# The bias of layer h in the joint part of a graph kernel: from products on TensorE to a column on ScalarE

## What is computed

```python
h = relu(layernorm(x))                       # x: 50000 x 256
S = h[src]                                   # 50000 edges
for r in (0, 1):                             # two relations
    msg_r = relu(relu(S @ W_r.T + b_r) @ W_r.T + b_r)
msgs = where(edge_type == r, msg_r)
agg  = segment_sum(msgs, dst)                # 50000 x 256
i, f, g, o = split(agg @ W_ih.T + b_ih + b_hh)
c  = sigmoid(i) * tanh(g)
hn = sigmoid(o) * tanh(c)
y  = relu(relu(hn @ W1.T + b1) @ W2.T + b2) @ W3.T + b3
out = x + y
```

## Time and profile before

| | |
|---|---|
| median of 3 runs | 2325.51 us (2324.17 to 2326.10) |
| time of the profiled execution | 2326.91 us |
| its span, first to last instruction | 2325.2 us |
| TensorE busy | 2098.4 us, 90% |
| VectorE busy | 1757.9 us, 76% |
| ScalarE busy | 1628.3 us, 70% |
| GpSimd busy | 1150.3 us, 49% |
| mean granted TensorE clock | 0.958 of full speed |

### The profile page before, as it was taken

The page is one execution under the profiler, slowest core; times in us unless marked ns, Lnnn a source line. Parts: engine busy times, 40 slices in busy tenths (PEclk is TensorE's granted clock), DMA queues, the critical chain, the costliest instruction groups (busy, mean ns, idle before and its releaser), DMA issues.

```text
span 2325.2 us, 51837 instructions
## 1 busy us (share of the span) xinstructions
PE 2098.4 (90%) x14224; PEld 1403.6 (60%) x14225; DVE 1757.9 (76%) x4311; ACT 1628.3 (70%) x3364; POOL 1150.3 (49%) x917
## 2 busy tenths in 40 slices
PE   6858777657999999999999999999999999999996
PEld 5747565545666666666666666666666666445553
DVE  7537655555788888888888888888888877788886
ACT  2437655546878787877878787878778786666663
POOL 0037777777555565555655556555555543100000
PEclk7559989999999999999999999999999999999998
DMA  9955555557699989989898989998988987998886
GB/s 387 425 180 100 98 98 96 98 93 143 124 175 171 167 170 170 172 171 172 167 172 172 174 166 169 171 172 172 167 172 169 174 156 151 182 193 188 188 188 154
DMA packets 400606, 396.90 MB, mean 171 GB/s; under 512 B 263738, under 2 KB 343158, under 8 KB 394360
## 3 DMA queue, kind: packets, MB, share of 16 engines
q0 software_dynamic: 91200, 157.34, 42.6%
q1 hardware_dynamic: 306788, 238.12, 40.0%
q10 hardware_dynamic: 2516, 0.14, 0.1%
HBM read 185.88 MB, written 156.97 MB: 147 GB/s over the span
## 4 chain that ended last, share of the span: by engine, by line
PE 43%; ACT 25%; issue 16%; POOL 6%; DVE 5%; DMA 4%; another core or an unknown queue 1%; POOLq 0%; SPq 0%; ACTq 0%; DVEq 0%
PE bank L1469 21%; ACT xn L757 4%; PE bank L1452 4%; PE bank L1483 3%; POOL agg L664 3%; PE bank L1416 3%; POOL xg L648 3%; ACT count_tmp L736 3%; ACT row_hi L790 2%; ACT tcell L783 2%; PE bank L1435 2%; PE bank L1508 2%; ACT g_o L777 2%; PE bank L1398 2%; DMA agg<-summed,scatter_idx 2%
## 5 line engine op out<-in xcount | busy, mean ns | idle before, releaser
L664 POOL DMA_INDIRECT agg<-summed,scatter_idx x400 | 638.2, 1596 | 599.7 <-DVE scatter_idx L1144 454.7
L1469 PE MATMUL bank<-a_hi,ihT 128*128 128x512 f16 x2400 | 715.6, 380 | 4.7 <-DMA a_lo<-row_lo 4.7
L648 POOL DMA_INDIRECT xg<-in_x,src_ring x400 | 416.1, 1040 | 270.2 <-DMA src_ring<-src_slot 137.3
L1469 PE MATMUL bank<-a_lo,ihT 128*128 128x512 f16 x1200 | 455.8, 380 | 0.0
L1469 PEld LDWEIGHTS bank<-a_hi,ihT 128*128 128x128 f16 x2400 | 235.0, 98 | 215.7 <-issue 7.2
L1435 PE MATMUL bank<-relT,h_hi 128*128 x1600 | 322.2, 276 | 0.0
L1416 PE MATMUL bank<-s_hi,relT 128*128 128x256 f16 x1600 | 294.8, 280 | 0.0
L672 POOL DMA_DIRECT2D y<-in_x x100 | 133.2, 1341 | 295.2 <-DVE y L1202 284.3
L777 ACT ACTIVATE g_i<-bank,gate_b 128x512 f32<-128x512 f32 x200 | 137.4, 687 | 138.7 <-PE bank L1469 133.3
L1416 PE MATMUL bank<-s_lo,relT 128*128 128x256 f16 x800 | 223.3, 279 | 0.0
L757 ACT ACTIVATE xn<-xg,shift,rstd 128x256 f32<-128x256 f32 x400 | 216.3, 591 | 9.3 <-DVE shift L1111 9.3
(11 more groups left out here) (197 smaller groups left out, 4647.7 us busy)
## 6 DMA issues: line engine op xcount, KB each, us to landing
agg_in<-agg SPq DMA_DIRECT2D x100, 512.0 KB
y<-in_x POOLq DMA_DIRECT2D x100, 512.0 KB, 6.5
out<-y SPq DMA_DIRECT2D x100, 512.0 KB
agg<-zeros SPq DMA_DIRECT2D x24, 2112.0 KB, 15.9
dst_ring<-dst_rows SPq DMA_DIRECT2D x200, 128.0 KB
xg<-in_x,src_ring POOLq DMA_INDIRECT x400
agg<-summed,scatter_idx POOLq DMA_INDIRECT x400
src_ring<-src_slot SPq DMA_DIRECT2D x200, 1.0 KB
```

Source lines behind the costliest of these rows:

```text
L648: nc.gpsimd.indirect_dma_start(out=xg[:, k.slot(8), t, :], out_offset=None, in_=x[:, :], in_offset=bass.IndirectOffsetOnAxis(ap=src_ring[: ...
L664: nc.gpsimd.indirect_dma_start(out=agg[:, :], out_offset=bass.IndirectOffsetOnAxis(ap=scatter_idx[:, k.slot(8), t:t + 1], axis=0), in_=sum ...
L1469: last = nc.tensor.matmul(N_C[c % 2][:, 0:UNIT], lhs, rhs, start=i == 0, stop=i == len(todo) - 1)
```

## The change

In the joint part `layer_h` no longer opens each half of its bank with a product of `brel_parts` and ones; the first of the six products opens it. ScalarE's `high_h` takes two instructions, one for each half of 256 columns, since the bias differs between them; each adds a bias column and applies the ReLU, and writes f32 to a new tile `h_f`. VectorE makes `h_hi` as a cast of `h_f` (a new `high_h` on VectorE) and `h_lo` as `h_f` less `h_hi`. VectorE's `low_h` moves behind `hidden`, and the new cast stands ahead of `hidden`. The columns are in `pair_bias`, two for each pair, which the set-up makes out of `pair_rel` (now on all 128 partitions) and `brel_col`, loaded by one more DMA on ScalarE's queue. TensorE frees the bank for the next pair on `h_f_ready` instead of `h_ready`. The edge part keeps its bias products. `brel_parts` is still used by layer m.

```diff
-WEIGHT_LOADS = 14
+WEIGHT_LOADS = 15
...
             act.dma_start(brel_row[:, :], b_rel.rearrange("r d -> (r d)").partition_broadcast(2)).then_inc(weights_in, 16)
+            act.dma_start(brel_col[:, :, :], b_rel.rearrange("r (c p) -> p r c", p=P)).then_inc(weights_in, 16)
...
             def high_h(k):
                 if k.within(PAIRS):
                     act.wait_ge(h_done, k.n + 1)
-                    nc.scalar.activation(h_hi[:, k.slot(2), :], B_H[k.bank][:, :], ACT.Relu).then_inc(h_hi_ready, 1)
+                    if k.both:
+                        if k.is_(NB):
+                            act.wait_ge(pair_bias_ready, 1)
+
+                        act.wait_ge(h_ready, k.n)
+                        for m in range(KH):
+                            half = slice(m * PAIR, (m + 1) * PAIR)
+                            last = nc.scalar.activation(h_f[:, half], B_H[k.bank][:, half], ACT.Relu,
+                                                        bias=pair_bias[:, bass.ds(k.n * KH + m, 1)])
+                        last.then_inc(h_f_ready, 1)
+                    else:
+                        nc.scalar.activation(h_hi[:, k.slot(2), :], B_H[k.bank][:, :], ACT.Relu).then_inc(h_hi_ready, 1)
...
-            alternate.then_inc(pair_rel_ready, 1)
+            chained(alternate)
+            nc.vector.tensor_scalar(other_rel[:, :], pair_rel[:, :], 0.0, None, ALU.is_equal).then_inc(pair_rel_ready, 1)
+            dve.wait_ge(pair_rel_ready, 1)
+            dve.wait_ge(weights_in, 16 * WEIGHT_LOADS)
+            for m in range(KH):
+                last = nc.vector.tensor_scalar(other_bias[:, :, m], other_rel[:, :], brel_col[:, 0, m:m + 1], None, ALU.mult)
+            chained(last)
+            bias_of = pair_bias[:, :].rearrange("p (n m) -> p n m", m=KH)
+            for m in range(KH):
+                last = nc.vector.scalar_tensor_tensor(out=bias_of[:, :, m], in0=pair_rel[:, :], scalar=brel_col[:, 1, m:m + 1],
+                                                      in1=other_bias[:, :, m], op0=ALU.mult, op1=ALU.add)
+            last.then_inc(pair_bias_ready, 1)
...
             def low_h(k):
                 if k.within(PAIRS):
-                    dve.wait_ge(h_hi_ready, k.n + 1)
-                    nc.vector.scalar_tensor_tensor(out=h_lo[:, k.slot(2), :], in0=B_H[k.bank][:, :], scalar=0.0,
-                                                   in1=h_hi[:, k.slot(2), :], op0=ALU.max,
-                                                   op1=ALU.subtract).then_inc(h_ready, 1)
+                    if k.both:
+                        dve.wait_ge(h_hi_ready, k.n + 1)
+                        nc.vector.tensor_tensor(h_lo[:, k.slot(2), :], h_f[:, :], h_hi[:, k.slot(2), :],
+                                                ALU.subtract).then_inc(h_ready, 1)
...
+            def high_h(k):
+                if k.within(PAIRS):
+                    dve.wait_ge(h_f_ready, k.n - NB + 1)
+
+                    wait_from(dve, m_done, k.n - 1)
+                    nc.vector.tensor_copy(h_hi[:, k.slot(2), :], h_f[:, :]).then_inc(h_hi_ready, 1)
...
+                if (at - 1).both:
+                    high_h(at - 1)
+                hidden(k, half)
                 low_h(at - 1)
-                hidden(k, half)
...
-                wait_from(pe, h_ready, k.n if k.both else k.n - 1)
+                if k.is_(NB):
+                    pe.wait_ge(h_ready, k.n)
+                elif k.both:
+                    pe.wait_ge(h_f_ready, k.n - NB)
+                else:
+                    wait_from(pe, h_ready, k.n - 1)
                 for m in range(KH):
                     ps = B_H[k.bank][:, m * PAIR:(m + 1) * PAIR]
-                    nc.tensor.matmul(ps, brel_parts[:, bass.ds(r * D + m * P, P)], ones16[:, :], start=True, stop=False)
+                    if not k.both:
+                        nc.tensor.matmul(ps, brel_parts[:, bass.ds(r * D + m * P, P)], ones16[:, :], start=True, stop=False)
...
-                        last = nc.tensor.matmul(ps, lhs, rhs, start=False, stop=i == len(todo) - 1)
+                        last = nc.tensor.matmul(ps, lhs, rhs, start=k.both and i == 0, stop=i == len(todo) - 1)
```

More of the change, by code:

```diff
@@ L218, in build @@
         spare_row = sb("spare_row", [P, 2])
-        pair_start = sb("pair_start", [1, PAIRS])
+        pair_start = sb("pair_start", [P, PAIRS])
         iota_tile = sb("iota_tile", [P, TILES])
@@ L228, in build @@
         dst_slot = sb("dst_slot", [P, TILES])
-        pair_rel = sb("pair_rel", [1, PAIRS], I32)
+        pair_rel = sb("pair_rel", [P, PAIRS], I32)
+        pair_bias = sb("pair_bias", [P, PAIRS * KH])
         unit_row = sb("unit_row", [1, UNITS], I32)
@@ L243, in build @@
         gate_b = sb("gate_b", [P, 8])
+        brel_col = sb("brel_col", [P, NUM_REL, KH])
         b1_col = sb("b1_col", [P, 1])
@@ L295, in build @@
         quarter_row = tmp("quarter_row", [1, QUARTERS])
-        flips = tmp("flips", [1, 2, PAIRS])
+        flips = tmp("flips", [P, 2, PAIRS])
+        other_rel = tmp("other_rel", [P, PAIRS])
+        other_bias = tmp("other_bias", [P, PAIRS, KH])
         slot = tmp("slot", [ROWS, COLS])
@@ L360, in build @@
         s_lo = sb("s_lo", [P, 2, KH * PAIR], F16)
+        h_f = sb("h_f", [P, KH * PAIR])
         h_hi = sb("h_hi", [P, 2, KH * PAIR], F16)
@@ L401, in build @@
         pair_rel_ready = sem("pair_rel_ready")
+        pair_bias_ready = sem("pair_bias_ready")
         unit_row_ready = sem("unit_row_ready")
@@ L430, in build @@
         h_done = sem("h_done")
+        h_f_ready = sem("h_f_ready")
         h_hi_ready = sem("h_hi_ready")
@@ L1010, in _ @@
                         lanes(i * BATCHES + b)
-            alternate = nc.vector.tensor_scalar(flips[:, 0, :], pair_start[:, :], base_s[0:1, QUARTERS - 1, 0:1], None, ALU.is_ge)
+            alternate = nc.vector.tensor_scalar(flips[:, 0, :], pair_start[:, :], base_s[:, QUARTERS - 1, 0:1], None, ALU.is_ge)
             for n, o in enumerate(range(QUARTERS - 2, -1, -1)):
@@ L1017, in _ @@
                 alternate = nc.vector.scalar_tensor_tensor(out=out_t, in0=pair_start[:, :],
-                                                           scalar=base_s[0:1, o, 1 - o % 2:2 - o % 2], in1=flips[:, n % 2, :],
+                                                           scalar=base_s[:, o, 1 - o % 2:2 - o % 2], in1=flips[:, n % 2, :],
                                                            op0=ALU.is_ge, op1=ALU.subtract)
-            alternate.then_inc(pair_rel_ready, 1)
+            chained(alternate)
[10 more added lines that the diff above has]
+            last.then_inc(pair_bias_ready, 1)
             chained(nc.vector.scalar_tensor_tensor(out=rows_of[:, :, :], in0=sel[0:1, :, :], scalar=float(QROWS),
@@ L1075, in low_h @@
                 if k.within(PAIRS):
-                    dve.wait_ge(h_hi_ready, k.n + 1)
-                    nc.vector.scalar_tensor_tensor(out=h_lo[:, k.slot(2), :], in0=B_H[k.bank][:, :], scalar=0.0,
-                                                   in1=h_hi[:, k.slot(2), :], op0=ALU.max,
-                                                   op1=ALU.subtract).then_inc(h_ready, 1)
+                    if k.both:
[3 more added lines that the diff above has]
+                    else:
+                        dve.wait_ge(h_hi_ready, k.n + 1)
+                        nc.vector.scalar_tensor_tensor(out=h_lo[:, k.slot(2), :], in0=B_H[k.bank][:, :], scalar=0.0,
+                                                       in1=h_hi[:, k.slot(2), :], op0=ALU.max,
+                                                       op1=ALU.subtract).then_inc(h_ready, 1)
+            def high_h(k):
[3 more added lines that the diff above has]
+                    nc.vector.tensor_copy(h_hi[:, k.slot(2), :], h_f[:, :]).then_inc(h_hi_ready, 1)
             def spread_of(k):
```

## The result

| | before | after |
|---|---|---|
| median of 4 runs | 2324.84 us (2322.63 to 2326.10) | 2349.99 us (2346.45 to 2353.19) |
| ratio, 95% interval | | 1.0103 (1.0080 to 1.0125) |
| span of the profiled execution | 2325.2 us | 2351.5 us |

The kernel became slower by 25 us. I had forecast 8 us, with 2349 as the upper edge; the median lies 1 us above it.

What follows compares the result with a forecast made beforehand. TensorE was taken to bound even steps, ScalarE odd ones; -15.4 us (TensorE) and +23.1 (ScalarE), the rest nothing, gave +7.7 us, 2333.2 us. The range ran from 2321 to 2349 us, the forecast's own from 2330 to 2338.

Steps and rivals of the forecast that it cites:

- What bounds the kernel: Joint part: even steps (9.99 us) end on TensorE, odd ones on ScalarE, which shows no idle time from `g_g` to `summed`.
- TensorE's term: Layer h, joint part: two matmuls fewer save 0.217 us in each of 71 even steps, -15.4 us; nothing in odd steps.
- ScalarE's term: Layer h's ReLU cut in two with a bias column: 0.33 us added in each of 70 odd steps, +23.1 us.
- the line through `g_i` and the root at 8 columns: Price of ScalarE's half-tile ReLU with bias: 0.59 and 0.21 us give 0.00075 us a column, so 0.40 us each.
- The errata table: ScalarE reading PSUM: 172 cycles plus one per column; second ReLU adds 143 ns, total -5.4 us; weighed, not followed.
- rival D: ScalarE's ReLU pair adds 0.15 to 0.29 us or partly finds cover: no change that can be told, 2321 to 2330 us; chance 0.22.
- The sign that I had set for being wrong: ScalarE's two ReLU halves following each other in under 0.35 us would show the forecast wrong.
- VectorE's step: VectorE: a cast added and `low_h` moved behind `hidden`, making later helpers 0.68 us late; claimed to cost nothing.
- Rival C: Every fourth step's boundary: ScalarE's table load waits for VectorE's `mean_var`, +24 us on top of 7.7, 2357 us; chance 0.09.
- Cost nothing: Verdict on VectorE's cast and moved `low_h`, on the new waits and on the set-up: no time added.
- A: ScalarE's ReLU pair: the bias column is free, 0.09 us added per odd step, -9.1 us, 2316 us; chance 0.11.
- B: ScalarE's ReLU halves cost what the `xn` pair costs, 0.52 us added per odd step, +21 us, 2346.5 us; chance 0.15.

## Why the prediction was right in its direction, and why its size was a third

*What bounds the kernel: right.* Even steps end on TensorE, odd ones on ScalarE; the runs with even steps only and with the products kept show both halves.

*TensorE's term: right.* Forecast 71 x 0.217 = -15.4 us; even steps went from 9.99 to 9.77.

*ScalarE's term: right in kind, over a third too large.* Forecast 0.33 added, measured 0.71 - 0.47 = 0.24; odd steps became 10.10 and 10.44 in place of 10.19 and 10.52, and the sums waited 0.82 us in place of 0.91. The mis-sized part is the line through `g_i` and the root at 8 columns: half a tile takes 0.71 / 2 = 0.355 us, not 0.40. The slope of 0.00075 us a column was too small: from 512 columns with a bias column (0.57) to 256 (0.355) it is 0.00084. The errata table that I had weighed (the Trainium skill, "VectorE: DVE Perf Modes") is right about the cut: 143 ns by its estimate, 0.14 measured. It has no term for the column, which cost 0.10 here; that is what I had held against it. With the measured price the sum is 70 x 0.24 - 15.4 = +1.4 us, which is rival D's case and not the forecast. The sign that I had set for being wrong here, halves that follow each other in under 0.35 us, was missed by less than 0.01.

*VectorE's step: the times right, the step wrong.* The cast, the move and the late helpers cost nothing in the steps that repeat, as said: the kernel with `low_h` ahead has the same ones. Rival C falls too. Timelines after, of ScalarE and of VectorE at a boundary:

```profile
1237.29 0.69 ACT L815 ACTIVATE x<-bank,b_col 128x512 f32<-128x512 f32 x1
1238.00 1.28 ACT L752 ACT_TABLE_LOAD   x1
1239.29 0.30 ACT L752 ACTIVATE std<-mean_var,eps 128x8 f32<-128x8 f32 x1
```

```profile
1238.27 0.24 DVE L1128 BATCH_NORM_AGGREGATE mean_var<-stats 128x2 f32<-128x6 f32 x2
```

The load starts 0.5 us before `mean_var` ends.

But the verdict "Cost nothing" on VectorE's work was reached by adding up durations, and it left out the number and the place of the instructions. 24 more in the loop and 40 more ahead of it moved its end from 0.20 to 0.70 of 128 behind a multiple, and that cost 21.9 us in 13 turns. No rival of mine had that; it was the step that failed. That the kernel got clearly slower, and that the time came near the upper edge, is luck: it is owed to a cause that I hadn't named. What I had named gives +1.4 us by the measured prices and +4.2 (0.7 to 7.7) by the timed runs without the stalls.

*The sum of the parts.* The spans differ by 26.3 us. The 17 groups of eight steps give 17 x 0.11 = 1.9, the fetching 21.9. Another 1.7 lies in the first eight steps of the joint part (81.83 us, with 11.07 in one step); the runs of the changed kernel with 32, 64 (both) and 128 memsets have that as well (81.81 to 81.85), the one with 192 (80.17) and the one with `low_h` ahead (80.15) have not. What makes it stays open. The rest, 0.8, is from before and after the joint part.

*Rivals.* A (the column is free) falls by 0.10 us. B (as dear as `xn`, 0.99) falls by 0.71. D was right for the change itself: it needed an added time of 0.15 to 0.29, and that was 0.24.

## What to carry to other kernels

Ask in which steps a saving and a cost fall before you add them: here the same edit is worth -0.22 us where TensorE ends the step and +0.24 us where ScalarE does, and doing it in every second step only turned a zero into a gain. When an edit changes the number of instructions ahead of or in a loop, look at the first instruction of the loop for idle time with no releaser and at the packets of the instruction queue, before you look for a cause in the edit; dummy instructions ahead of the loop show in a run or two whether it is the place (64 took the stall away here, 32 and 128 didn't). And a kernel can be slower for its layout alone: the unchanged one got 13 stalls, and 12 us in the steps that have them, from 64 memsets in idle time.

## What the runs showed of the hardware

The stall at the jump back of VectorE's loop depends on the place of the loop with a period of 128 instructions: loops that ended at numbers 1562, 1594, 1690 and 1818 of the program (0.20, 0.45, 0.20 and 0.20 of 128 behind a multiple) had none; those that ended at 1626 (twice), 1658 and 1754 (0.70, 0.95, 0.70) had it at all 13 jumps. In the changed kernel it was 49.6 / 13 = 3.8 us on average, 4.4 at most, and 1.0 to 2.2 us of that reached the step (0.3 to 1.3 in the kernel before with 64 memsets). A packet of this queue was 0.93 MB / 113 = 8.2 KB, which at the compiled program's 64 bytes an instruction is 128 instructions, and a stalling loop fetched 5 of them a turn. The Trainium skill, "Runtime: NRT & Kernel Launch", section on instruction fetch, says that a taken branch whose target has left the engine's buffer waits for a DMA; the runs agree. It gives blocks of 256 instructions, which is the size of q8's packets (0.90 MB / 55 = 16.4 KB); on q14, and for VectorE's stall, 128 is the measured one. Whether the loop's end or its beginning decides wasn't separated. ScalarE's loop grew too (202 to 233 instructions) and showed no such idle time.
